# Attention slots: the rounding of the rows of squares moved ahead of the copy of u (ScalarE) and ahead of the two caps (VectorE)

## The reference, cut to what matters

```
xn = _ln(x, ln_scale)
Q, K, V = xn @ W_q, xn @ W_k, xn @ W_v            # per head
q2 = sum(Q * Q, -1)[..., :, None]
k2 = sum(K * K, -1)[..., None, :]
sqdist = maximum(q2 + k2 - 2.0 * einsum('bhsf,bhtf->bhst', Q, K), 0.0)
scores = exp(-gamma * sqdist)
out = einsum('bhst,bhtf->bhsf', scores, V)
out.transpose(0, 2, 1, 3).reshape(B, S, H * E) @ W_o.T
```

## Time and profile before

| | |
|---|---|
| time, median of 3 runs | 820.28 us (820.22 to 820.9) |
| the profiled execution's own time | 819.13 us |
| its span, first to last instruction | 817.3 us |
| busy: TensorE matmul / VectorE / ScalarE / GpSimd | 763.8 / 626.8 / 539.1 / 463.9 us |
| attention part | from about 95 to 500 us of the span |
| one attention step | 25.3 us |
| mean granted clock of the TensorE | 0.98 |

### The profile page before, as it was taken

How to read it: one execution, slowest core, us unless ns; L and a number is a source line. 1 busy time by engine, 2 the same in 40 slices (tenths; PEclk the granted TensorE clock), 3 DMA queues, 4 the chain that set the end, 5 groups by cost and what they waited for, 6 DMA issues and landing times.

```text
span 817.3 us, 16809 instructions
## 1 busy us (share of the span) xinstructions
PE 763.8 (93%) x5712; PEld 448.9 (55%) x5712; DVE 626.8 (77%) x1537; ACT 539.1 (66%) x1058; POOL 463.9 (57%) x628
## 2 busy tenths in 40 slices
PE   2999889999999999999999998999999999999993
PEld 1343456666666666666666665454555554545441
DVE  3677668778887788887887875888888888888861
ACT  1465578888888888888888886444455555455432
POOL 8740255545446454464454541366777777777766
PEclk9999979999999999999999998999999999999996
DMA  6300022111221112211122111000000000000000
GB/s 163 117 2 2 2 52 53 27 40 40 52 53 27 39 40 53 53 37 37 33 53 53 44 35 27 1 3 6 10 7 8 8 8 11 11 9 7 9 7 20
DMA packets 22860, 25.71 MB, mean 31 GB/s; under 512 B 12888, under 2 KB 21720, under 8 KB 22648
## 3 DMA queue, kind: packets, MB, share of 16 engines
q1 hardware_dynamic: 21608, 23.57, 12.3%
q10 hardware_dynamic: 1168, 1.07, 0.6%
HBM read 5.30 MB, written 2.43 MB: 9 GB/s over the span
## 4 chain that ended last, share of the span: by engine, by line
PE 74%; DVE 16%; issue 5%; POOL 2%; ACT 2%; ACTq 1%; DMA 1%; POOLq 0%; SPq 0%; DVEq 0%
PE bank L1059 14%; PE bank L1107 11%; PE bank L1083 9%; PE bank L1085 7%; PE bank L1195 7%; PE bank L1174 6%; PE bank L987 6%; DVE gated L912 4%; PE bank L1111 3%; PE bank L1228 2%; DVE top L894 2%; PE bank L977 2%; DVE top L898 1%; DVE lg L885 1%; PE bank L1220 1%
## 5 line engine op out<-in xcount | busy, mean ns | idle before, releaser
L782 DVE TENSOR_SCALAR prob<-prob,cap_hi,cap_lo 125x500 f32<-125x500 f32 x256 | 156.3, 637 | 50.7 <-ACT prob L539 48.6
L405 POOL TENSOR_TENSOR sq<-sq 125x256 f32<-125x256 f32 x128 | 97.6, 773 | 156.0 <-ACT sq L553 132.5
L539 ACT ACTIVATE prob<-bank 125x500 f32<-125x500 f32 x256 | 148.9, 592 | 40.7 <-PE bank L1085 38.8
L1195 PE MATMUL bank<-gated,w_sb 64*64 64x500 f32 x1024 | 164.4, 586 | 0.0
L1174 PE MATMUL bank<-cs,w_sb 64*64 64x500 f32 x1024 | 161.5, 581 | 1.7 <-DVE gated L912 1.6
L442 POOL TENSOR_TENSOR gated<-relu,wb 128x500 f32<-128x500 f32 x96 | 119.9, 1249 | 71.3 <-ACT relu L633 71.2
L912 DVE SCALAR_TENSOR_TENSOR gated<-bank,nb,wb 128x500 f32<-128x500 f32 x160 | 115.6, 732 | 41.9 <-PE bank L1174 41.7
L633 ACT ACTIVATE relu<-bank,b_sb 128x500 f32<-128x500 f32 x96 | 64.6, 673 | 98.2 <-PE bank L1174 98.2
L1059 PE MATMUL bank<-prob,u 125*64 125x250 f32 x1024 | 124.5, 384 | 0.5 <-DVE prob L782 0.5
L1083 PE MATMUL bank<-m,s 128*125 128x500 f32 x256 | 111.4, 435 | 7.9 <-issue 6.9
L797 DVE TENSOR_TENSOR m<-bank,m 64x500 fp32r<-64x500 f32 x128 | 86.4, 675 | 27.5 <-ACT m L548 26.2
(11 more groups left out here) (169 smaller groups left out, 1356.3 us busy)
## 6 DMA issues: line engine op xcount, KB each, us to landing
m<-m SPq DMA_DIRECT2D x128, 125.0 KB, 2.3
out<-res SPq DMA_DIRECT2D x16, 125.0 KB
xa<-xparts SPq DMA_DIRECT2D x4, 281.2 KB
w_sb<-in_w SPq DMA_DIRECT2D x1, 1024.0 KB
xw<-xparts SPq DMA_DIRECT2D x4, 140.6 KB
w_sb<-in_w SPq DMA_DIRECT2D x1, 512.0 KB
m<-s SPq DMA_DIRECT2D x32, 15.6 KB
xparts<-x_part SPq DMA_DIRECT2D x1, 375.0 KB, 4.6
```

The costliest lines, as they stand in the source:

```text
L405: gp.tensor_tensor(sq2[q][:, :, :], sq[q][:, :, 0:D // 2], sq[q][:, :, D // 2:D], ALU.add)\
L539: act.activation(prob[v % PROBS][:, :, c, :], bank[5 + n % 3][0:T, 0:C].rearrange("p (h l) -> p h l", h=2), ACT.Exp).then_inc(b_exp, 1)
L782: dve.tensor_scalar(part, part, cap_hi[0:T, h:h + 1], cap_lo[0:T, h:h + 1], ALU.min, ALU.max)\
L1195: last = pe.matmul(y[cols, 0:C], w2_sb[rows, g, :], gated[g % 8][rows, :], start=g == 1 and rows is HI, stop=v == 7, skip_group_check=True)
```

## The change

In slot 5, ScalarE's rounding of the rows of squares (`rank_rows`, before at the end of the slot) is called ahead of unit 11, the copy of u. On VectorE the low parts of these rows are made ahead of the two caps of the slot, behind unit 10. Nothing is added or left out; the waits are the same, and the programs of the TensorE, GpSimd and the sync engine are as before.

```diff
@@ ScalarE
+            def rank_rows(p):
+                act.wait_ge(b_qt, p + 1)
+                wait(act, b_s2, p)
+                act.activation(rnd2[64:S_ROWS, :], bank[0][64:S_ROWS, 0:C], ACT.Copy).then_inc(b_rnd2, 1)
+
             def step_b(p, j, old2, old, new, ln):
...
                     for c in range(2):
                         if old:
                             exps(v, c)
+                        if new and v == 5 and c == 1:
+                            rank_rows(p)
                         if rest:
                             unit(rest.pop(0))
...
                     for k in rest:
                         unit(k)
-                    if new and v == 5:
-                        act.wait_ge(b_qt, p + 1)
-                        wait(act, b_s2, p)
-                        act.activation(rnd2[64:S_ROWS, :], bank[0][64:S_ROWS, 0:C], ACT.Copy).then_inc(b_rnd2, 1)
@@ VectorE
+                def rank_rows():
+                    dve.wait_ge(b_rnd2, p + 1)
+                    dve.scalar_tensor_tensor(s2[j][64:S_ROWS, :], f32(rnd2[64:S_ROWS, :]),
+                                             c_sb[64:S_ROWS, C_MS2:C_MS2 + 1], bank[0][64:S_ROWS, 0:C],
+                                             ALU.mult, ALU.add).then_inc(b_s2, 1)
+
...
                         if rest:
                             unit(rest.pop(0))
+                        if new and v == 5 and c == 0:
+                            rank_rows()
                         if old:
                             caps(v, c)
                     for k in rest:
                         unit(k)
                     if v == 2 and old2:
                         residual(p - 2, 0)
-                    if new and v == 5:
-                        dve.wait_ge(b_rnd2, p + 1)
-                        dve.scalar_tensor_tensor(s2[j][64:S_ROWS, :], f32(rnd2[64:S_ROWS, :]),
-                                                 c_sb[64:S_ROWS, C_MS2:C_MS2 + 1], bank[0][64:S_ROWS, 0:C],
-                                                 ALU.mult, ALU.add).then_inc(b_s2, 1)
```

## The result

| | before | changed |
|---|---|---|
| median of 6 runs | 820.32 us (819.16 to 820.9) | 823.97 us (822.86 to 824.36) |
| ratio | | 1.004, 95% interval 1.003 to 1.005 |
| span of the profiled execution | 817.3 us | 822.6 us |
| granted clock of the TensorE, mean | 0.98 | 0.98 |

The change makes the kernel 3.65 us slower, 0.4%. The prediction was 823.7 us.

The account below looks back on a forecast made before the run. TensorE's matmuls were taken to bound the attention part, with short stops. 15 x 0.29 = 4.35 us lost less 14 x 0.07 = 0.98 us returned, +3.4 on 820.28, gave 823.7 us; 8-in-10 range 820.8 to 827.0.

Parts of the forecast that it names:

- What ends the stop: Before a step's first scores on TensorE: the last exponential ends the 0.49 us wait; the rows have 0.8 us in hand.
- ScalarE: 0: ScalarE in slot 5: rounding and the copy of u change places at no cost, u 0.75 us later.
- VectorE: caps 0.77 us later, 0.45 us of it beyond the load: Slot 5's caps end 0.77 us later, making the weight load of slot 6's second half of products 0.45 us late.
- The price, 0.29 us a step: Slot 6's block of products grows by 0.07 + 0.22 = 0.29 us in each of 15 steps.
- slot 0's row: Slot 0's block of products: a load 0.23 us late lengthens it by only 0.07 us, from 1.84 to 1.91.
- What passes on: From slot 6 to the next step: the full 0.29 us passes on; slot 0's block gives back 0.07 us.
- The 0.49 us stop: TensorE's idle wait before a step's first scores, 14 times, 6.9 us in all; claimed not to absorb the 0.29 us.
- The sum: Whole kernel: 4.35 us lost less 0.98 us returned is +3.4 us, giving 823.7 us, 0.4% slower; chance 0.78.
- Rows that bound: Rival at the stop before the first scores: the rows end it, so 3.5 us faster, 816.8 us; chance 0.05.
- no change: Rival at slot 6's load: caps slip less or TensorE tolerates more, price some 0.1 us a step, 821 us; chance 0.10.
- the port: Rival: slot 5's caps fall on GpSimd's work on SBUF, adding 0.2 to 0.6 us a step, say 829 us; chance 0.07.

Follow-up runs that it names:

- Run 3: On the kernel before, the sync engine sends unit 12's duplicates first and the two rows of squares behind them; 827.11 us, ratio 1.0086.
- run 7: On the kernel before, slot 7's two exponentials go ahead of unit 14's copies and its two caps ahead of unit 14's subtraction; 810.31 us, ratio 0.9881.
- run 1: The changed kernel with VectorE's low parts back behind the caps, so only ScalarE's part of the change; 820.35 us, ratio 1.0003.
- runs 6: The changed kernel with the low parts made twice ahead of the caps, and GpSimd's centring made to wait for slot 5's two caps; 833.09 us, ratio 1.0157.
- run 5: The changed kernel with the low parts made twice ahead of the caps, first into a tile nobody reads then; 839.99 us, ratio 1.0247.
- run 2: The changed kernel with ScalarE's rounding back at the end of the slot, so only VectorE's part of the change; 827.03 us, ratio 1.0087.
- run 4: The changed kernel with the low parts in two halves, one ahead of the caps and one behind them; 819.36 us, ratio 0.999.

## Why the prediction was right

- **What ends the stop.** The step that decided the sign was that `b_exp`, not `b_row`, ends the stop before the first scores, although the profile names the DMA in the last step. Run 3 measured the row's reserve at 0.82 us (0.8 was said), run 7 removed the stop by moving the exponential, and in the changed kernel the last step's stop is 1.00 us still, with the DMA no longer named.
- **ScalarE: 0.** Shown by run 1.
- **VectorE: caps 0.77 us later, 0.45 us of it beyond the load.** Shown: both.
- **The price, 0.29 us a step.** Shown: 2.13 against 1.84 us in the chain's count. The doses make one curve: the load late by 0.17, 0.23, 0.45 and 0.76 us costs 0.01 to 0.02, 0.07, 0.29 and 0.60 us, and in runs 6 and 5 a load late by 1.10, 1.40 and 1.84 us costs 0.94, 1.25 and 1.68. So about 0.16 us are free, where the prediction said 0.2 and took the price from slot 0's row, which made the rounding harmless.
- **What passes on.** The 0.49 us stop did not absorb it, as said: both of its ends moved. Slot 0 gave back 0.07. The reason given was a little off: slot 7's caps were to move by 0.04 us and moved by 0.13, since the pair of caps in slot 6 now takes 1.92 us in place of 1.79. GpSimd's L387 had waited for slot 5's cap (0.39 us, before 0.20) and `xn` came 0.13 later. The return survived because 0.07 us of lateness is inside what the loads have free.
- **The sum.** +3.4 us forecast; +3.65 between the medians, whose interval is 2.5 to 4.1 us. The traces, step by step, give 3.4.
- **The rivals.** Rows that bound, no change, and the port: none happened here. The last was real and lay one further delay away (runs 5 and 6). The Trainium skill (SBUF — State Buffer, Who interferes with whom) says that whoever issues first has the shared pair for its whole instruction, and the other waits. Where the starts lie 0.2 us apart the traces agree: with the change the second cap of slot 5 starts 0.20 us ahead of L387, which takes 0.39 us in place of 0.20, and in run 2 it starts 0.22 us ahead of L367, which takes 0.79 us in place of 0.62. In run 5 the starts lie 0.1 us apart, and the rule cannot be read from them: the first cap is recorded first in every step, and in every second one it is that cap that is held, while L367 runs its 0.62 us.

## What to carry to other kernels

A wait with several conditions has one that ends last; find it by timing each against the start of the waiter, not by the name that the profile gives, and prove it by delaying the one and moving the other. An instruction moved ahead of others on an in-order engine must be paid by those, so ask for the slack of what it displaces: here 0.32 us until the caps were waited for and 0.16 us of tolerance, against a delay of 0.77. What was made earlier had 0.8 us to spare; the exponential that really held the step was worth 10.5 us.

## What the runs showed of the hardware that had not been expected

- VectorE and GpSimd on SBUF couple the engines in ways that only an exact position shows: two caps of 0.99 us the pair take 1.72 and 1.29 us in turn beside GpSimd's centring, with starts that agree to 0.01 us, and an added wait on GpSimd gave 6.6 us back (runs 5 and 6). GpSimd's power (125x4) takes 1.25 us where a cap has started 0.17 us before it and 1.01 us where it starts 0.34 us ahead of the caps (the kernel before and run 4).
- The weight loads of a running block were free up to about 0.16 us of lateness (0.17 us late cost 0.01 to 0.02); beyond that all of it counted, up to the 1.84 us of run 5.
